# A gated cross-attention and mixture-of-experts block: the gate in four products, the experts' biases in one rounded product, VectorE's chains in single pieces

## The reference

```python
x = x + jnp.tanh(g_xattn[0]) * _L0_xattn_ref(_layernorm(x, axis=-1), ctx_1024, ctx_1024, mask, ...)
x = x + jnp.tanh(g_ffn[0]) * _L0_ffn_ref(_layernorm(x, axis=-1), ...)
...
# inside _L0_ffn_ref, behind the attention:
x1 = _layer_norm(x + attn_out, ln1_w, ln1_b)
gates = jax.nn.softmax(x1 @ gate_w.T + gate_b, axis=-1)
_, top_idx = jax.lax.top_k(gates, TOP_K)
top_gates = jnp.take_along_axis(gates, top_idx, axis=-1)
expert_outputs = jnp.einsum('bsd,efd->bsef', x1, expert_w) + expert_b[None, None]
sel = jnp.take_along_axis(expert_outputs, top_idx[..., None], axis=2)
moe_out = jnp.sum(sel * top_gates[..., None], axis=2)
return _layer_norm(x1 + moe_out, ln2_w, ln2_b)
```

## Time and profile before

| what | value |
| --- | --- |
| median of 3 runs | 911.13 us (907.36 to 911.41) |
| profiled execution | 909.4 us, span 907.5 us |
| PE busy | 829.5 us, 91% |
| DVE busy | 717.2 us, 79% |
| ACT busy | 561.0 us, 62% |
| POOL busy | 471.4 us, 52% |
| granted clock of PE, mean | 0.98 |

### The profile page before, as it was taken

How to read it: one execution, slowest core, us unless ns; L and a number is a source line. 1 busy time by engine, 2 the same in 40 slices (tenths; PEclk the granted TensorE clock), 3 DMA queues, 4 the chain that set the end, 5 groups by cost and what they waited for, 6 DMA issues and landing times.

```text
span 907.5 us, 23558 instructions
## 1 busy us (share of the span) xinstructions
PE 829.5 (91%) x9316; PEld 633.2 (70%) x9316; DVE 717.2 (79%) x1940; ACT 561.0 (62%) x1267; POOL 471.4 (52%) x851
## 2 busy tenths in 40 slices
PE   3667999999999999999999999999999999999764
PEld 2445777777777777777777777777777777777543
DVE  2456888888888888888888888888888888888663
ACT  3467666676677666766676666766776667666320
POOL 5025546555566556555565555555665565554532
PEclk9988899999999999999999999999999999999997
DMA  7310000000000000000000000000000000000000
GB/s 210 99 38 14 14 2 21 21 21 21 20 15 7 21 21 20 21 21 21 20 8 14 21 21 21 20 20 21 13 9 20 21 20 8 8 8 7 7 7 12
DMA packets 33821, 21.19 MB, mean 23 GB/s; under 512 B 11560, under 2 KB 33584, under 8 KB 33712
## 3 DMA queue, kind: packets, MB, share of 16 engines
q1 hardware_dynamic: 33712, 19.69, 7.6%
HBM read 15.49 MB, written 4.19 MB: 22 GB/s over the span
## 4 chain that ended last, share of the span: by engine, by line
PE 62%; DVE 21%; POOL 9%; ACT 3%; issue 2%; DMA 1%; SPq 1%; POOLq 0%
PE bank L346 32%; PE bank L463 8%; PE bank L445 7%; POOL rope_tmp L1004 4%; PE bank L502 3%; PE bank L355 3%; POOL roped L1002 3%; POOL roped L1008 3%; DVE equals L883 2%; PE bank L513 2%; PE bank L356 2%; DVE beats L885 2%; PE bank L432 2%; DVE o_t_A_b L745 1%; DVE stats_B L732 1%
## 5 line engine op out<-in xcount | busy, mean ns | idle before, releaser
L916 DVE SCALAR_TENSOR_TENSOR moe<-bank,gates,moe 128x256 f32<-128x256 f32 x256 | 123.4, 482 | 63.1 <-PE bank L346 58.3
L969 POOL TENSOR_SCALAR var_eps<-mean_var 128x1 f32<-128x1 f32 x64 | 12.2, 191 | 293.8 <-DVE mean_var L734 293.8
L346 PE MATMUL bank<-w_expertsa,u_t_a 128*128 128x512 f32 x256 | 108.8, 425 | 3.4 <-DVE moe L916 3.4
L624 ACT ACTIVATE bank<-mask_add 128x512 f32<-128x512 bf16 x128 | 76.6, 602 | 46.9 <-DVE neg_max_A L818 46.9
L346 PE MATMUL bank<-w_expertsb,u_t_a 128*128 128x512 f32 x256 | 102.3, 400 | 0.0
L346 PE MATMUL bank<-w_expertsa,u_t_b 128*128 128x512 f32 x256 | 102.2, 399 | 0.0
L1052 POOL TENSOR_SCALAR_AFFINE_SELECT probs_B<-probs_B 128x512 f32<-128x512 f32 x128 | 77.0, 637 | 35.2 <-ACT probs_B L658 31.1
L818 DVE TENSOR_REDUCE neg_max_A<-bank 128x4 f32<-128x512 f32 x128 | 79.2, 681 | 3.5 <-PE bank L445 3.5
L818 DVE TENSOR_REDUCE neg_max_B<-bank 128x4 f32<-128x512 f32 x128 | 79.2, 680 | 0.1
L658 ACT ACTIVATE probs_A<-bank 128x512 f32<-128x512 f32 x128 | 66.1, 604 | 11.5 <-PE bank L484 11.5
L615 ACT ACTIVATE bank<-causal_add 128x512 f32<-128x512 bf16 x128 | 69.8, 625 | 0.0
(11 more groups left out here) (209 smaller groups left out, 2455.2 us busy)
## 6 DMA issues: line engine op xcount, KB each, us to landing
x_in<-in_x SPq DMA_DIRECT2D x32, 128.0 KB, 2.3
ctx_t<-in_ctxT SPq DMA_DIRECT2D x32, 128.0 KB, 2.7
out<-y_out SPq DMA_DIRECT2D x32, 128.0 KB, 1.7
w_stage<-in_expertsT SPq DMA_DIRECT2D x8, 256.0 KB, 3.9
mask_u<-in_masks SPq DMA_DIRECT2D x32, 32.0 KB, 2.2
w_stage<-in_in_projT SPq DMA_DIRECT2D x3, 256.0 KB, 7.4
w_stage<-in_WkT SPq DMA_DIRECT2D x1, 256.0 KB, 2.8
w_stage<-in_WvT SPq DMA_DIRECT2D x1, 256.0 KB, 3.0
```

What stands on the lines that cost most here:

```text
L346: done = pe.matmul(out_ap, l, r, start=n == 0, stop=n == len(terms) - 1)
L624: act.activation(score_banks[g][:].rearrange("p (h k) -> p h k", k=P), mask_add[t % MASK_SLOTS][:, 1:2, :].to_broadcast([P, GROUP, P]), AC ...
L916: dve.scalar_tensor_tensor(out=moe[(e + 1) % 2][:], in0=bank[:, (e % 2) * EMBED:(e % 2 + 1) * EMBED], scalar=gates[:, e:e + 1], in1=moe[e ...
```

## The change

The gate's weights hold both parts side by side, 16 columns, so that two parts of u in two chunks make four products instead of six; the two halves are added on DVE. The experts' biases are multiplied in one rounded product: the gates stand in three strips of 32 rows, with the low part of the gates in the second and the low part of the biases in the third. DVE's norm statistics, reciprocals and expert sums become calls of their own and are laid out anew among other work. All five loops are reordered. The uses of the three banks get fixed banks instead of turns, and waits that others imply are dropped. x gets six slots and the context five instead of four and three. The gains are loaded first and tanh is ACT's first instruction. `LATER` begins in round 0 with six matrices.

```diff
-X_SLOTS = 4
-CTX_SLOTS = 3
+X_SLOTS = 6
+CTX_SLOTS = 5
...
-LATER = ((), ("Ak", "Av", "Aq"), ("Ao", "Bk", "Bq"), ("Bv", "Bo", "E0", "E1", "E2"), ("E3", "E4", "E5", "E6", "E7"))
+LATER = (("Ak", "Av", "Aq", "Ao", "Bk", "Bq"), ("Bv", "Bo", "E0", "E1", "E2"), ("E3", "E4", "E5"), ("E6", "E7"))
...
-    ("pair3", 5, (("moe", 9, 9),)),
+    ("pair3", 1, 4, (("moe", 9, 9),)),
...
+            for n, g in enumerate(("g_xattn", "g_ffn")):
+                load_row(gains[:, n:n + 1], dram[g], "ld_gains")
             load_x(0)
...
-            sp.dma_start(expert_bias[0:EXPERTS, :], dram["L0_ffn_expert_b"]).then_inc(sem["ld_rows"], 16)
+            for n in range(3):
+                sp.dma_start(bias_f[n * STRIP:n * STRIP + EXPERTS, :], dram["L0_ffn_expert_b"]).then_inc(sem["ld_rows"], 16)
...
-                products(bank[:, 0:EXPERTS], [chunk(u_t, c) for c in range(CHUNKS)],
-                         [tuple(w[:, c, :] for w in gate_w) for c in range(CHUNKS)]).then_inc(sem["gate_mm"], 1)
+                steps = [(part, c) for c in range(CHUNKS) for part in u_t]
+                for n, (part, c) in enumerate(steps):
+                    done = pe.matmul(bank[:, 0:2 * EXPERTS], chunk((part,), c)[0],
+                                     gate_w[:, c, :, :].rearrange("p a e -> p (a e)"), start=n == 0, stop=n == len(steps) - 1)
+                done.then_inc(sem["gate_mm"], 1)
...
-                pe.wait_ge(sem["gates_t"], t + 1)
+                pe.wait_ge(sem["gates_t_b"], t + 1)
                 bank = work_bank("bias", t)
                 pe.matmul(bank[:, 0:EMBED], gates_t[:], expert_bias[:], start=True, stop=True).then_inc(sem["bias_mm"], 1)
...
+                expert_pair(0, r - 3)
+                project_o("B", r - 2)
+                project_qk_b(r - 1)
+                transpose_max("A", r)
+                scores_t("A", r)
+                subtract_max("A", r)
+                expert_pair(1, r - 3)
+                heads_transposed("B", "q", r - 1)
+                expert_pair(2, r - 3)
+                heads_transposed("B", "k", r - 1)
...
                 if r == 1:
-                    act.wait_ge(sem["ld_gains"], 32)
-                    act.activation(tanh_gains[:], gains[:], ACT.Tanh)
-                if r == 3:
-                    act.wait_ge(sem["ld_rows"], 16 * 8)
-                    act.activation(gate_w[0][:], gate_f[:], ACT.Copy)
-
+                    act.wait_ge(sem["ld_rows"], 16 * 10)
+                    act.activation(gate_w[:, :, 0, :], gate_f[:], ACT.Copy).then_inc(sem["w_gate_a"], 1)
+                    act.activation(expert_bias[:], bias_f[:], ACT.Copy).then_inc(sem["w_bias_a"], 1)
+
+            act.wait_ge(sem["ld_gains"], 32)
+            act.activation(tanh_gains[:], gains[:], ACT.Tanh)
...
-                dve.tensor_tensor(logits[:], work_bank("gate", t)[:, 0:EXPERTS], gate_bias[:], ALU.add).then_inc(
-                    sem["logits"], 1)
+                bank = work_bank("gate", t)
+                dve.tensor_tensor(logits[:], bank[:, 0:EXPERTS], gate_bias[:], ALU.add).then_inc(sem["logit_a"], 1)
+                dve.wait_ge(sem["logit_a"], t + 1)
+                dve.tensor_tensor(logits[:], logits[:], bank[:, EXPERTS:2 * EXPERTS], ALU.add).then_inc(sem["logits"], 1)
...
+            def gates_low(t):
+                if not live(t):
+                    return
+                low = slice(STRIP, 2 * STRIP)
+                dve.wait_ge(sem["gates_t"], t + 1)
+                dve.tensor_tensor(gates_t[low, :], work_bank("gates_t", t)[low, 0:P], gates_t[low, :].bitcast(F32),
+                                  ALU.subtract).then_inc(sem["gates_t_b"], 1)
...
+                mask_of_tile(r)
+                inverse_root("1", r - 4, "un")
+                base_b(r - 3)
+                base_a(r - 2)
+                scale_shift_u(r - 4)
+                for g in range(GROUPS):
+                    causal(g, r - 3)
+                inverse_root("B", r - 2, "yn")
+                rope(r - 2)
+                inverse_root("2", r - 5, "vn")
+                finish(r - 5)
                 context_parts(r)
                 inverse_root("A", r, "xn")
```

More of the change, by code:

```diff
@@ new lines @@
+    ("A_k", 2, 0, (("A_kh", 2, 2),)),
+    ("B_normalise", 1, 2, (("B_on", 1, 1),)),
+    ("A_q", 0, 0, (("A_qh", 1, 1),)),
+    ("gates_t", 2, 3, (("gates_t_b", 1, 1),)),
+    ("B_o_t", 1, 2, (("B_ot_b", 1, 1),)),
+    ("rope_t", 0, 1, (("rope_t_b", 1, 1),)),
+    ("bias", 2, 3, (("moe", 9, 1),)),
+    ("pair0", 1, 3, (("moe", 9, 3),)),
+    ("B_out", 0, 2, (("B_res", 1, 1),)),
+    ("B_qk", 2, 1, (("B_qk_f", 1, 1),)),
+    ("A_max_t", 0, 0, (("A_mt", 1, 1),)),
+    ("pair1", 1, 3, (("moe", 9, 5),)),
@@ L73 @@
+    ("B_q", 2, 1, (("B_qh", 1, 1),)),
+    ("pair2", 0, 3, (("moe", 9, 7),)),
+    ("B_k", 2, 1, (("B_kh", 2, 2),)),
 )
@@ L305, in sync_program @@
             load_tile(1)
-            for n, g in enumerate(("g_xattn", "g_ffn")):
-                load_row(gains[:, n:n + 1], dram[g], "ld_gains")
             load_row(rows["bo_A"][:], row_src["bo_A"], "ld_bo_A")
@@ L429, in heads_transposed @@
                 first = EMBED * "qk".index(w)
-                bank = (take_work if tag == "A" else work_bank)(f"{tag}_{w}", t)
+                bank = (take_work if tag == "B" else work_bank)(f"{tag}_{w}", t)
                 for c in range(CHUNKS):
@@ L578, in tensor_program @@
[L578 to L587 removed]
+                expert_pair(3, r - 4)
+                x_t(r)
+                u_transposed(r - 3)
+                scores("B", r - 2)
@@ new lines, in tensor_program @@
+                attend("A", r - 1)
+                y_transposed(r - 2)
+                gate(r - 3)
+                normalise("A", r - 1)
+                scores_t("B", r - 2)
+                transpose_max("B", r - 2)
+                o_transposed("A", r - 1)
+                subtract_max("B", r - 2)
+                project_v_b(r - 2)
+                project_o("A", r - 1)
+                project_kv_a(r)
+                attend("B", r - 2)
+                project_q_a(r)
+                heads_transposed("A", "k", r)
@@ L728, in later, with statistics, mean_variance @@
                         split_low(m)
-            def norm_stats(n, t, src, used):
-                dve.bn_stats(stats[n][:], src[:]).then_inc(sem["st_" + n], 1)
+            norm_of = {"A": (lambda t: x_in[t % X_SLOTS], "xn"), "B": (lambda t: x1[t % X1_SLOTS], "yn"),
+                       "1": (lambda t: u_n, "un"), "2": (lambda t: moe[0], "vn")}
+            def statistics(n, t):
+                if not live(t):
+                    return
+                if n == "A":
+                    dve.wait_ge(sem[f"ld_x{t % X_SLOTS}"], slot_loads(t, X_SLOTS))
+                if n == "B":
+                    dve.wait_ge(sem["A_res"], t + 1)
+                if n == "2":
+                    dve.wait_ge(sem["moe"], 9 * t + 9)
+                dve.bn_stats(stats[n][:], norm_of[n][0](t)[:]).then_inc(sem["st_" + n], 1)
+            def mean_variance(n, t):
+                if not live(t):
+                    return
                 dve.wait_ge(sem["st_" + n], t + 1)
@@ L809, in add_values @@
                     src = work_bank("B_v", t)[:, 0:EMBED]
+                if t == 0 and tag == "A":
+                    dve.wait_ge(sem["ld_rows_" + tag], 48 if tag == "A" else 64)
                 dve.tensor_tensor(values[tag][:, :, 0:HEAD_DIM], by_head(src), by_head(rows["bv_" + tag][:]),
@@ L840, in normalise @@
                     sem[tag + "_inv"], 1)
+            def normalise(tag, t):
+                if not live(t):
+                    return
+                heads = work_bank(tag + "_normalise", t)[:].rearrange("p (h s) -> p h s", s=STRIP)
                 dve.wait_ge(sem[tag + "_inv"], t + 1)
```

281 lines of the change are left out of this document (117 added, 164 removed).

## The result

The changed kernel takes 923.8 us (median of four runs, 922.1 to 928.8), the kernel before 911.3 us in the same comparison. The ratio is 1.0147, with a 95% interval of 1.012 to 1.0174. The profiled execution took 925.36 us with a span of 923.3, so it is 15.8 longer in span than the one before (907.5).

The account below looks back on a forecast made before the run. PE limits only the half-tile behind the rotated y; DVE, ACT and POOL set most of the other half's pace. Profiled 909.4 + 5.4 (start) + 5.1 (30 tiles) - 0.5 (end) = 919.4, called 920 us; range 903 to 934.

Parts of the forecast that it names:

- The start: First rounds: early weight splits make the first scores 9.6 us later, 4.2 comes back; +5.4, bounds +1 to +9.
- bias product: PE, between the rotated y and A's scores: the rounded product costs 0.17 us a tile, the exact one was hidden.
- pair 3's bank: Expert products: u_n between the sums of experts 2 and 3 frees the bank late; loss 0 to 0.3, taken 0.15.
- Rival B: Settled tiles: the period stays at 25.64, only the start is lost; 916, or 912 with early loads; chance 0.18.
- rival D: The start is given back whole by later rounds with fewer splits, period falls by 0.1; 909; chance 0.06.
- Gate products: PE, ahead of the o_raw transposition: two fewer products gain 0 us a tile, bound 0.05.
- rival A: PE's work counts everywhere: 0.63 us off each of 30 tiles, 19 in all; 897; chance 0.12.
- v_n and the maxima of A: DVE behind the rotation: v_n takes about 0.8, maxima start at 516.86 instead of 516.37, still in time; cost 0.
- B bias: DVE's bias addition for B ends near 523.0, just when pair 1 ends and PE wants the query heads.
- rival C: DVE becomes the limit behind the rotation: maxima of A at 517 or later, +0.6 a tile; 934; chance 0.12.
- VectorE's chain: DVE's way to yn: B's values between A's residual and its statistics save two seams, 0.11 us a tile.
- The end: Last tile: pair 0 before B's output product saves about 0.5 us.

Follow-up runs that it names:

- e1: Changed kernel with the weight-split table of the kernel before and the gate and bias roundings back in round 3; ratio 1.0083, 917.7 us.
- e4: Kernel before with only the four-product gate and the second logit addition on DVE; ratio 1.0039, period 25.78.
- e7: e2's kernel without the product of the gates with the experts' biases; ratio 0.9982, period 25.63.
- e2: Changed kernel with POOL's addition of ln2_b moved from beside v_n to ahead of the causal selects; ratio 1.004, 914.0 us.
- e11: Control: kernel before with POOL's addition of base_B moved from beside u_n to ahead of its root; ratio 1.0001, period 25.68.
- e6: e2's kernel with ACT writing B's key heads after two of its four causal seeds; ratio 1.0000, period 25.62.
- e3: Changed kernel with DVE's bias addition of B's queries and keys ahead of the application of xn; ratio 1.0124, 921.5 us.
- e9: Kernel before with A's residual ahead of B's values on DVE and the statistics of x1 behind both; ratio 0.9956, period 25.56.
- e10: Changed kernel with B's values ahead of A's residual on DVE again; ratio 1.0152, 926.2 us.
- e5: Changed kernel with B's output product ahead of pair 0 and u_n ahead of the sum of expert 2; ratio 1.0121, 922.4 us.

## Why the prediction was right, and which sizes were off

The direction and the two places (start and settled stretch) were right, and the time (923.8) lies in the range of 903 to 934, 3.8 above the forecast of 920. The start was right in its mechanism. In the settled stretch the sign was right by luck: the two terms that made it a loss, the bias product and pair 3's bank, turned out to be worth almost nothing, and the loss came from a place that the prediction had put at 0. Rival B (the period stays) is out by 26.00 against 25.67, and rival D (the start is given back whole) by the 5 us at the fifth tile. Step by step:

**The start, forecast +5.4, measured about +5** (5.15 at the fifth tile and 5.19 at the transposed scores that the prediction named; 5.4 between the means of all traces of either start). The mechanism is shown by e1. That the size fits so well is partly luck, since its parts were off: xn_t_a came at 25.7 and not 28.3, because the third expert matrix landed before 25 and not at 27.4, and of the 7.8 at the first scores 2.6 were given back and not the 4.2 forecast.

**Gate products, forecast 0: right.** e4 shows the two products worth nothing, so rival A falls in this part. In e4 the second logit addition costs 0.10 where it stands in front of o_norm_A, and there the prediction had no entry for it.

**Bias product, forecast +0.17: too much.** It measures 0.06 in a settled tile (e7, on top of e2). Its 0.31 to 0.35 on PE are larger than the bounds of 0.13 to 0.22, but they lie beside v_n. The step that failed is "in the half where PE is the limit": after the change it no longer was.

**v_n and the maxima of A, forecast 0: this is where the loss is. Undoing it gives back 0.32 of 0.33 (e2).** The smaller losses (B bias 0.10, the bank of the key heads 0.06, bias product 0.06) and the gain ahead of the rotated y, below, then cancel, since e2's period is that of the kernel before. The prediction had v_n at 0.8 (measured 0.73) behind POOL's root, beside finish. It failed at the sentence that the maxima "still come in time, with 0.0 to 0.1 to spare". I had v_n 0.76 behind the start of the transposition of the rotated y (515.46 - 514.70). It is 499.52 - 498.57 = 0.95. From v_n to the maxima I had 1.40, and it is 1.51. Together the maxima start 2.46 behind the rotated y instead of 2.16, and their transposition missed PE by 0.29. The margin was smaller than the error of the estimate. This is rival C's mechanism at half its price.
The Trainium skill (SBUF — State Buffer, "Who interferes with whom") describes the lock of the shared port pair. e2 and e11 agree with it: v_n falls from 0.73 to 0.41 and u_n from 0.82 to 0.41 when POOL's instruction is moved away.

**Pair 3's bank, forecast 0.15: nothing.** Its products follow the key heads without a gap (509.08, 509.21). In its place stands a wait that I had not seen, of the transposition of u for the bank of B's key heads. Taken away on top of e2 it is worth 0.06 (e6). The B bias, which the prediction had end just when PE wants the query heads, is 0.2 late, and taking that away is worth 0.10 (e3).

**VectorE's chain, forecast -0.11: right in the kernel before, nothing in the changed one.** e9 measures 0.11 for the order in the kernel before. Undoing the same order in the changed kernel moves the period by 0.02 (e10). The step that failed is that POOL's root follows DVE's mean and variance: in the changed kernel it follows the last causal select. The half from xn to the rotated y is still 0.30 shorter. Up to the transposed scores of B it is 0.25 longer (4.56 instead of 4.31), and from the first select to the root it is 0.50 shorter (2.54 instead of 3.04). So the gain is that DVE's statistics no longer hold the root. What brought them forward was read from the traces and not tested alone: the order is one part, and another is that the multiplication of equals by lower_tri takes 0.22 at 518.03, starting just ahead of POOL's first causal select (518.06), and 0.65 at 507.82 in the kernel before, behind that select's start (507.76).
The Trainium skill (VectorE: DVE Perf Modes, "The DRAIN you can't avoid") finds no extra cost of a semaphore after each of eight copies; by that, as the prediction read it, the seam would be 0. The same section also says that a next instruction that is not held starts earlier. e9 shows 0.11 for the order, and the measurement decides.

**The end, forecast -0.5: not confirmed.** The pair of traces gives +1.8, within the spread of that stretch, so the change there as a whole is not shown. The reason that the forecast gave does not hold: pair 0 ahead of B's output product saves no 0.5, it puts u_n 2.5 and the last u 1.6 later (e5).

**The sum.** The forecast adds 10.0 to the span, and the pair of traces differs by 15.8. Settled tiles make 3.8 of the difference (8.9 instead of 5.1), the end 2.3 and the start -0.25. Only the first is firm. It is v_n and the maxima, put at 0. Two small slips in the sum itself: its 0.04 of small gains stands on no row, and 919.4 with the 1.7 added would be 921, not 920.

What stays open: what brought DVE's statistics forward was only read, not tested; e5's and e3's gains in time are within the overlap of the intervals; and 3.5 us of what e7 saves have no place.

## What to carry to other kernels

Where a chain comes out with less than 0.1 us to spare, treat it as lost: one addition on GpSimd in the wrong place cost 9.8 us of 924. Price an instruction by what waits behind it in the new order, not by the engine that was the limit in the old one: a product of 0.35 on PE was worth 0.06 in a settled tile, 0.32 of DVE time on v_n was worth 0.32, and 0.41 on u_n nothing. When weight splits are put ahead of the first tile, expect most of their time to be paid: here the first scores were 6.6 late against e1, and the fifth tile still was. And before a difference at the start or the end of a program is explained, read the same stretch in several traces: here it differed by 3 to 6 us between traces with the same order there, while a settled tile repeated within 0.02.

## What was not expected of the hardware

- A DVE instruction that starts within a POOL instruction can be stretched until about the end of that one: the first xn took 1.95 and one weight split 2.50 at 18 to 23 us of the changed kernel, while POOL filled the large pick table, against 0.41 and 0.67 elsewhere. Both ended 0.2 to 0.5 behind the POOL instruction that they had started in.
- DVE's product of two SBUF tiles (equals by lower_tri) took 0.65 when it started 0.06 behind POOL's select and 0.22 when it started 0.03 ahead of it.
- PE's granted clock at the end was 0.50 over 880 to 890 of the changed kernel and 0.66 over the next ten us, with pauses of 0.6 to 3 us on PE in each tile of the end; half of the last expert products ran at 0.43 us each instead of 0.23.
